# Output kept by tokens, decays as sums of logarithms, and elementwise work moved to GpSimd in an attention and Mamba kernel

## The chip, the cores and the metric

One core of one Trainium2 chip runs the kernel. The metric is the device time in microseconds (us) of one execution. The engines are named here TensorE (PE, with its weight loads PEld), VectorE (DVE), ScalarE (ACT), GpSimd (POOL) and SyncE (SP, which issues the transfers).

## The reference

The input `x` is (4, 128, 32, 32) in float32: four batches of 128 channels by 1024 tokens. Two blocks follow one another.

```
# block 1: attention
h = group_norm(x, 8 groups)                  # per batch
q, k, v = h @ qkv_w.T + qkv_b                # 1024 tokens x 128
x = x + softmax(q k^T / sqrt(128)) v @ proj_w.T + proj_b
# block 2: Mamba-2 with squeeze-and-excitation
u = layer_norm(x over channels)
z, xBC, dt = u @ in_w.T                      # 128, 128+64+64, 4
xs, B, C = silu(causal_conv4(xBC));  dt = softplus(dt + dt_bias)
state = state * exp(dt*A) + dt * xs * B;  y = state . C + Dp * xs   # 4 heads of 32
y = y * silu(z);  y = y * rsqrt(mean(y*y) + eps) * rms_w
out = y @ out_w.T
att = sigmoid(relu(mean_tokens(out) @ se1.T + b1) @ se2.T + b2)
result = x + out * att
```

## The kernel before

Everything stays on chip between the input and the output. A batch's 1024 tokens are worked in two halves of 512 (index `n`, 0 or 1), each of four tiles of 128 tokens. In a step's name the digits are the half, the tile or the sub-step, the letter is the batch (a to d), and `@k` the matmul bank that it fills. One list, `ORDER`, written out in the source, names every step once. Each engine walks the whole list and issues the steps that are its own; semaphores (`wait`) carry the data dependences. So the list sets each engine's queue, and an engine serves its queue strictly in order.

**Attention.** `h` (normalized input), `h_hi` and `h_lo` (a split into two reduced-precision parts) and `q_hi`, `q_lo` feed three-product matmuls: `Q`, and `S` (scores, 128 x 512). `max`, `exp`, `T` (transpose), `pT` (copy), `PV` (product with the values), `inv` and `res` (division and addition to the residual, which lies by tokens in `res`) follow. `xob` adds the projection's bias to `res` beforehand. `h_lo` and `xob` run on VectorE.

**Mamba.** `stats`, `ln_ve`, `ln_pow`, `u_tok`, `UT` and `u` make the normalized tokens; `InX`, `InBC`, `InZ` and `Dt` project them; `conv_x` and `conv_bc` are four taps each; `sp0` to `sp17` are the softplus in nine small VectorE steps per half, the last of which gives `la`, the logarithm of the decay. The decay of one step is `dA = exp(la)`. It is split into two parts and put into rows (`dA_rows`), transposed (`DAT`), masked by head (`dA_T`), spread by `L` over a bank, and `l`, a scan on VectorE, multiplies it up. `Dec` computes the sums of `la` up to each token with 16 products of 32 columns, and `decay` takes their exponential. `G`, `m`, `U`, `st`, `stc`, `Yo`, `Y` are the chunked state recurrence; `y` adds its parts; `g` applies the gate.

**End of a batch.** `sq`, `Ss`, `ms`, `y_pow` give `y_rstd`, one number a token. The output is by channels, so that number has to become a row: `y_rows` (two VectorE steps), `YrT` (transpose), `y_T` (copy), `YrB` (four products), `y_b` (copy). `Out` is one 128 x 512 product; `o` multiplies it by `y_b` and sums it over the tokens. `SeA`, `hdn`, `SeB`, `tha`, `att` are the excitation. `XR` transposes the residual back to channels and `fin` adds it, into `y`, from where SyncE stores 256 KB a half. The next batch's `y` waits for that store:

```
elif kind == "y":
    wait(dve, yo_dx_ready, b, n + 1)
    wait(dve, out_sent[n], b - 1, 16)
```

GpSimd has `ln_pow`, `gate`, `xend`, `dx`, `yo_dx`, `g` and `y_pow`. The order staggers the batches: while batch b is in its Mamba part, the attention of batch b+1 runs; after the last attention, only Mamba is left. At the start the statistics of batches 1 to 3 (`gn_stats1`) stand in VectorE's queue between `h_lo1a` and `q_lo0a`, and `winC` is made (`win_mm`) before `Q0a`.

## Time and profile before

| | |
|---|---|
| median of 3 runs | 328.7 us (328.65 to 328.84) |
| the profiled execution's own time | 328.64 us |
| its span, first to last instruction | 326.9 us |
| mean granted TensorE clock | 0.974 |
| busy: PE, DVE, ACT, POOL | 284.5, 261.0, 187.3, 81.9 us |
| instructions | 6452 |

Busy time is the union of an engine's instructions. Matmuls are pipelined, and a record also covers its latency, so TensorE's busy time is more than its throughput needs; how far apart equal products start in a dense stretch is the better price. A float32 product appears as two records, a transpose or a reduced-precision product as one.

### The profile page before, as it was taken

The page shows a single profiled execution, that of the slowest core. Times are in us where ns is not written, and L with a number is a line of the kernel's source. Part 1 is how long each engine was busy: PE and PEld are TensorE (multiplying, and loading weights), DVE is VectorE, ACT ScalarE, POOL GpSimd, SP SyncE. Part 2 cuts the span into 40 slices and gives each one's busy share as a digit, 9 for nine tenths or more (in the row PEclk, how much of TensorE's full clock was granted, in tenths as well). Part 3 has the DMA queues.
Part 4 walks back from the last instruction along what each step waited for, and adds up shares of the span by engine and source line. Part 5 has one row for each costly group of instructions (what it writes and reads, how often), then busy time and mean ns, then how long its engine had stood idle before and what let it go on. Part 6 is the DMA issues. An engine that isn't in the chain of part 4 may idle for free.

```text
span 326.9 us, 6452 instructions
## 1 busy us (share of the span) xinstructions
PE 284.5 (87%) x2206; PEld 232.1 (71%) x2206; DVE 261.0 (80%) x586; ACT 187.3 (57%) x347; POOL 81.9 (25%) x99
## 2 busy tenths in 40 slices
PE   0598999999999999899999999999999988756663
PEld 0477897897879778676787877887987765445542
DVE  4674475997798978969989998988999988996523
ACT  1324577978786855666587656566574835641011
POOL 6000100001011025541502522162023176107340
PEclk9999999999999999999999999999999999996777
DMA  7900000000000000000000000000000010000101
GB/s 216 369 6 1 2 0 3 0 2 0 2 1 3 0 2 2 0 3 1 2 1 9 25 34 1 2 0 3 3 0 2 2 64 1 3 0 2 64 0 66
DMA packets 3791, 7.34 MB, mean 22 GB/s; under 512 B 656, under 2 KB 1584, under 8 KB 3760
## 3 DMA queue, kind: packets, MB, share of 16 engines
q1 hardware_dynamic: 3216, 6.72, 5.7%
q8 instruction: 19, 0.31, 0.4%
q10 hardware_dynamic: 544, 0.21, 0.2%
q14 instruction: 12, 0.10, 0.1%
HBM read 4.83 MB, written 2.10 MB: 21 GB/s over the span
## 4 chain that ended last, share of the span: by engine, by line
PE 57%; DVE 26%; issue 7%; ACT 4%; POOL 2%; DMA 2%; DVEq 1%; ACTq 0%; POOLq 0%
PE mamba L947 20%; PE attn_out L947 12%; PE scores L947 12%; PE turn L1015 6%; DVE L L872 4%; DVE pre L822 3%; DVE neg_max L784 3%; PE turn L947 2%; DMA out<-y 2%; DVE gn_raw L707 1%; PE mamba L1073 1%; DVE scanned L892 1%; DVE L L884 1%; DVE y L936 1%; DVE y L907 1%
## 5 line engine op out<-in xcount | busy, mean ns | idle before, releaser
L947 PE MATMUL attn_out<-values,pT 128*128 128x129 f32 x512 | 66.8, 276 | 0.3 <-DVE res L793 0.2
L947 PEld LDWEIGHTS attn_out<-values,pT 128*128 128x128 f32 x512 | 62.9, 191 | 4.2 <-issue 2.8
L533 ACT ACTIVATE probs<-scores,neg_max 128x512 f32<-128x512 f32 x64 | 42.8, 684 | 25.8 <-DVE neg_max L784 20.4
L784 DVE TENSOR_REDUCE neg_max<-scores 128x1 f32<-128x1024 f32 x32 | 39.0, 1218 | 15.5 <-PE scores L947 15.1
L539 ACT ACTIVATE pT<-turn 128x512 f32<-128x512 f32 x64 | 37.4, 594 | 14.4 <-PE turn L1015 8.9
L872 DVE TENSOR_TENSOR_SCAN L<-mamba,ident 128x512 f32<-128x512 f32 x32 | 38.2, 1212 | 2.3 <-PE mamba L947 2.1
L1015 PE MATMUL turn<-ident,probs 128*128 128x128 f32 x256 | 37.8, 273 | 0.0
L822 DVE SCALAR_TENSOR_TENSOR pre<-raw,vec,pre 128x512 f32<-128x512 f32 x48 | 37.5, 789 | 0.2
L947 PE MATMUL scores<-h_hi,q_hi 128*128 128x512 f32 x64 | 31.4, 491 | 3.4 <-ACT probs L533 2.5
L1015 PEld LDWEIGHTS turn<-ident,probs 128*128 128x128 f32 x256 | 30.2, 141 | 5.8 <-issue 3.3
L445 POOL TENSOR_TENSOR ln_rstd<-ln_var,neg_half 128x4 f32<-128x4 f32 x8 | 8.5, 1066 | 81.1 <-DVE ln_var L804 81.1
L463 POOL TENSOR_TENSOR xend<-xdt,to_end 128x512 f32<-128x512 f32 x8 | 9.8, 1228 | 74.3 <-DVE xdt L865 39.0
L947 PE MATMUL scores<-h_hi,q_lo 128*128 128x512 f32 x64 | 25.8, 404 | 0.0
L947 PE MATMUL mamba<-u,winC 128*128 128x512 f32 x48 | 24.9, 604 | 0.9 <-DVE L L872 0.4
L947 PE MATMUL scores<-h_lo,q_hi 128*128 128x512 f32 x64 | 25.6, 400 | 0.0
L884 DVE TENSOR_TENSOR L<-L,mamba 128x512 f32<-128x512 f32 x32 | 21.3, 678 | 1.0 <-PE mamba L947 1.0
L456 POOL TENSOR_TENSOR gate<-gate,zv 128x512 f32<-128x512 f32 x16 | 20.5, 1286 | 3.6 <-ACT gate L584 3.4
L947 PEld LDWEIGHTS scores<-h_hi,q_hi 128*128 128x128 f32 x64 | 12.3, 192 | 11.1 <-issue 7.6
L947 PE MATMUL mamba<-dA_head,pick_chunk 128*128 128x512 f32 x32 | 14.3, 468 | 2.4 <-ACT BT L616 0.6
L623 ACT ACTIVATE stateT<-scanned 128x512 f32<-128x512 f32 x8 | 9.2, 1145 | 12.1 <-DVE scanned L892 12.1
L484 POOL TENSOR_TENSOR xs<-y,gate 128x512 f32<-128x512 f32 x8 | 11.0, 1380 | 13.8 <-DVE y L907 13.8
L947 PEld LDWEIGHTS scores<-h_hi,q_lo 128*128 128x128 f32 x64 | 12.3, 192 | 2.9
(189 smaller groups left out, 572.1 us busy)
## 6 DMA issues: line engine op xcount, KB each, us to landing
res<-in_x_tok SPq DMA_DIRECT2D x4, 512.0 KB, 8.1
out<-y SPq DMA_DIRECT2D x8, 256.0 KB, 2.0
x_all<-in_x SPq DMA_DIRECT2D x3, 512.0 KB, 8.0
x_all<-in_x SPq DMA_DIRECT2D x2, 256.0 KB, 3.2
winT<-in_in_wT SPq DMA_DIRECT2D x1, 194.0 KB, 6.4
wqkv<-in_qkv_w ACTq DMA_DIRECT2D x1, 192.0 KB, 3.6
wpT<-in_proj_wT SPq DMA_DIRECT2D x1, 64.0 KB, 3.6
ob_row<-in_proj_b SPq DMA_DIRECT2D x1, 64.0 KB, 5.5
```

The source lines that it names most:

```text
L456: pool.tensor_tensor(gate[:, half], gate[:, half], zv[:, half], ALU.add if part else ALU.mult).then_inc(gate_ready.sem, 1)
L463: pool.tensor_tensor(xend[:, rows, :], xdt[:, rows, :], to_end[:, rows].unsqueeze(2).broadcast_to([P, R, HEADDIM]), ALU.mult).then_inc(xen ...
L484: pool.tensor_tensor(y2[:, half], y[:, half], gate[:, half], ALU.mult).then_inc(y2_ready.sem, 1)
L533: act.activation(probs[:, i % 2, half_of(h)], scores[:, half_of(h)], ACT.Exp, bias=neg_max[:, i:i + 1]).then_inc(exp_done.sem, 1)
L539: act.activation(pT[:, i % 2, QUAD * h:QUAD * (h + 1), :], bank[:, :].rearrange("p (a b) -> p a b", a=QUAD), ACT.Copy).then_inc(pT_ready.s ...
L623: act.activation(stateT[:, n, :, :], scanned[:, n, :, :].rearrange("s e c -> s c e"), ACT.Copy).then_inc(stc_ready.sem, 1)
L784: V.tensor_reduce(neg_max[:, n:n + 1], scores[:, :], AX.X, ALU.max, negate=True).then_inc(max_ready.sem, 1)
L822: V.scalar_tensor_tensor(pre[:, k, half_of(n)], raw[:, k, n * HALF + j:(n + 1) * HALF + j], vec[:, at + j:at + j + 1], pre[:, k, half_of(n ...
L872: V.tensor_tensor_scan(L[:, HEADS * n:HEADS * (n + 1), :].rearrange("p a b -> p (a b)"), bank[:, :], ident4[:, :, :].rearrange("p a b -> p ...
L884: V.tensor_tensor(M[:, HEADS * n:HEADS * (n + 1), :], L[:, HEADS * n:HEADS * (n + 1), :], bank[:, tile(c)].unsqueeze(1).broadcast_to([P, H ...
L947: return T.matmul(o, w, v, start=start, stop=stop)
L1015: last = T.transpose(bank[:, tile(c)], probs[:, i % 2, tile(QUAD * h + c)], ident[:, :])
```

## The change

The output by tokens. `Out` becomes four products that put tokens on the partitions, so `y_rstd` is one number a partition: `o` is four scaled copies on ScalarE. `y_rows`, `YrT`, `y_T`, `YrB`, `y_b`, `XR` and `att` go. The mean over tokens is now `os` (GpSimd adds pairs of tiles), `Pl` (two products with ones) and `pl` (a copy). `SeB` gives the excitation broadcast over the partitions, with its bias as a 33rd row; `gated` (VectorE) multiplies, into the spent `x_all`; `fin` adds it to `res`, on GpSimd for batches 0 to 2 and on VectorE for the last; the store goes from `res`, 256 KB a half with 2 KB pieces a partition as before, and the host puts the result back by channels.

The decays. `Cum` computes the sums of `la` for the 16 columns with one product, `dec` takes the exponential on ScalarE, and it travels in `dA_rows` beside `dA`, through `DAT` and `dA_T`; `Dec` is then one product 512 wide with `head_sel`, and `decay` is a copy. `cd` reads its sums from `Cum`'s bank.

VectorE's work on GpSimd: `xob` and `h_lo` for batches 1 to 3.

The head: `gn_bs1` to `gn_bs3` are the statistics in three pieces; `win_mm` comes after `S1a`; `kq_mm` after `gn_mm20`; the whole order is a new one. A kind `warm`, products on idle TensorE, is defined, but the order does not contain it.

```
 ORDER = """
+gn_stats0 gn_mm10 vp_mm gn_dev0 gn_mm20 kq_mm gn_ve0 vp_ev gn_pow0 gn_aff0 win_s h_hi0a xob0a h0a h_hi1a h_lo0a h1a
+kq_ev Q0a h_lo1a V0a@0 q_hi0a gn_bs3 Q1a q_lo0a q_hi1a gn_bs1 S0a v0a V1a@1 q_lo1a v1a gn_bs2 S1a win_mm max0a
+gn_stats1 exp0a gn_mm11 exp1a S2a T0a@1 S3a pT0a T1a@1 max1a PV0a pT1a gn_dev1 PV1a exp2a exp3a T2a@1 alog S4a win_ev
...
+max6c L0b@2 PV5c stats0c exp12c Yo1a@0 inv2c l0b exp13c S14c yo1a S15c h_hi0d res2c yo_dx1a L1b@2 pT9c max7c Y1a@1
+h_hi1d h_lo0d L2b@0 th_bc1b PV6c exp14c silu1b PV7c pT10c y1a l1b th_x1b InZ1b@1 g1a stats1c L3b@2 xs0b h_lo1d zv1b
+Q0d stats2c zt1b inv3c T11c@1 res3c gate0b l2b Cum1b@1 exp15c PV8c dec1b q_hi0d dA_rows1b Q1d stats3c pT11c l3b PV9c
...
+yo_dx0d U1d@1 m4d dx1d st1d fin0c m5d stc1d Y0d@1 m6d Yo1d@2 y0d m7d g0d yo1d Y1d@2 yo_dx1d sq0d Out0d@1 y1d Ss0d@2
+g1d ms0d y_pow0d sq1d Ss1d@0 o0d ms1d Out1d@0 y_pow1d os0d o1d Pl0d@2 pl0d os1d fin1c Pl1d@0 pl1d SeA0d@1 hdn0d
+SeB0d@0 tha0d gated0d gated1d fin0d fin1d
@@ setup on VectorE
+            rows = ident[:, 0:4 * R].rearrange("r (s k c h) -> r k s c h", s=2, k=2, c=QUAD)
+            for k in range(2):
+                V.tensor_reduce(row_head[:, k, :], rows[:, k].rearrange("r s c h -> r h s c"), AX.XY, ALU.add)
+                last = V.tensor_reduce(row_chunk[:, k, :], rows[:, k].rearrange("r s c h -> r c s h"), AX.XY, ALU.add)
+            V.tensor_copy(head_sel[:, :, :], row_head[:, 1, :].unsqueeze(2).broadcast_to([P, HEADS, HEADDIM]))
+            step_done(V.tensor_tensor(head_mask[:, :, 1:P], row_head[:, 0, :].unsqueeze(2).broadcast_to([P, HEADS, P - 1]),
+                                      row_chunk[:, 1, :].unsqueeze(2).broadcast_to([P, HEADS, P - 1]), ALU.add))
@@ GpSimd
+                elif kind == "xob" and b > 0:
+                    pool.tensor_tensor(res[:, b, four, :], res[:, b, four, :],
+                                       ob_row[:, :].unsqueeze(1).broadcast_to([P, QUAD, P]), ALU.add
+                elif kind == "h_lo" and b > 0:
+                    pool.tensor_tensor(h_lo[:, half], h32[:, half], h_hi[:, half].bitcast(F32), ALU.subtract
+                elif kind == "os":
+                    pool.tensor_tensor(o_sum[:, n, :, :], o_tok[:, QUAD * n:QUAD * n + 2, :],
+                                       o_tok[:, QUAD * n + 2:QUAD * (n + 1), :], ALU.add)
+                elif kind == "fin" and b < BATCH - 1:
+                    pool.tensor_tensor(res[:, b, four, :], res[:, b, four, :], gated(b, n), ALU.add
@@ ScalarE
-                    act.activation(decay_in[:, half], bank[:, :], ACT.Exp, scale=1.0 / A_SCALE
+                    act.activation(decay_in[:, half], bank[:, :], ACT.Copy)
+                elif kind == "dec":
+                    act.activation(dA[:, n, R:2 * R], bank[:, 0:R], ACT.Exp, scale=1.0 / A_SCALE)
-                elif kind == "y_b":
+                elif kind == "o":
+                    for c in range(QUAD):
+                        last = act.activation(o_tok[:, i, :], bank[:, tile(c)], ACT.Copy, scale=y_rstd[:, i:i + 1])
@@ VectorE
                 elif kind == "y":
-                    wait(dve, out_sent[n], b - 1, 16)
+                    wait(dve, gated_ready, b - 1, n + 1)
+                    wait(dve, o_sum_ready, b - 1, n + 1)
+                elif kind == "gated":
+                    V.scalar_tensor_tensor(gated(b, n), th_att[:, :].unsqueeze(1).broadcast_to([P, QUAD, P]), 1.0,
+                                           o_tok[:, QUAD * n:QUAD * (n + 1), :], ALU.add, ALU.mult)
@@ TensorE
-                        for h in range(HEADS):
-                            last = mm(bank[h * HEADDIM:(h + 1) * HEADDIM, tile(c)],
-                                      la[:, n, r:r + 1].broadcast_to([P, HEADDIM]), upto[:, :])
+                elif kind == "Cum":
+                    mm(bank[:, 0:R], upto[:, :], la[:, n, :])
+                    mm(bank[:, R:2 * R], ones[:, :], la[:, n, :]).then_inc(done, 1)
+                elif kind == "Dec":
+                    mm(bank[:, :], head_sel[:, :, :].rearrange("r h d -> r (h d)"),
+                       dA_head[:, n, :, :].rearrange("r h i -> r (h i)")).then_inc(done, 1)
-                    mm(bank[:, :], woutT[:, :], y2[:, half]).then_inc(done, 1)
+                    for c in range(QUAD):
+                        last = mm(bank[:, tile(c)], y2[:, tile(QUAD * n + c)], woutT[:, :])
+                elif kind == "Pl":
+                    mm(bank[:, 0:1], o_sum[:, n, 0, :], ones[:, 0:1], True, False)
+                    mm(bank[:, 0:1], o_sum[:, n, 1, :], ones[:, 0:1], False, True).then_inc(done, 1)
-                elif kind == "XR":
```

## Rows read from the trace of the kernel before

**Rows 1.** The page: busy time of each engine, share and instructions.

```profile
PE 284.5 (87%) x2206; PEld 232.1 (71%) x2206; DVE 261.0 (80%) x586; ACT 187.3 (57%) x347; POOL 81.9 (25%) x99
```

**Rows 2.** Busy time by stretch: window, length, each engine's busy us, clock, DMA share, GB/s.

```profile
27.80:72.00 44.20, 42.56 (x312) 36.74 (x313) 30.59 (x81) 31.83 (x58) 1.87 (x2) 1.00 0.00 1
72.00:115.80 43.80, 43.10 (x286) 35.96 (x285) 36.99 (x78) 33.77 (x64) 3.57 (x3) 1.00 0.01 1
115.80:187.70 71.90, 67.56 (x602) 55.53 (x601) 64.03 (x132) 47.81 (x88) 26.67 (x24) 1.00 0.02 5
187.70:262.00 74.30, 72.26 (x608) 60.78 (x608) 68.35 (x159) 47.06 (x90) 19.37 (x18) 1.00 0.02 5
262.00:290.00 28.00, 22.41 (x202) 14.77 (x200) 25.07 (x58) 14.96 (x30) 12.40 (x10) 1.00 0.06 20
290.00:327.00 37.00, 21.28 (x154) 15.96 (x154) 18.90 (x37) 5.42 (x10) 12.00 (x12) 0.77 0.08 29
```

**Rows 3.** The chain that ended last, in the head: start, us, what.

```profile
17.18 3.58 DVE gn_raw L707 x6
21.78 1.50 PE scores L947 x3
...
24.92 1.63 PE scores L947 x3
...
28.67 0.94 PE scores L947 x3
```

**Rows 4.** The same chain in dense stretches, for the spacing of products.

```profile
123.22 0.87 PE turn L1015 x8
...
154.75 0.70 PE scores L947 x3
155.45 0.86 PE mamba L947 x2
...
158.41 1.08 PE mamba L947 x32
```

**Rows 5.** Groups of VectorE instructions: busy us, mean ns; idle before, releaser.

```profile
L936 DVE SCALAR_TENSOR_TENSOR y<-y,att,mamba 128x512 f32<-128x512 f32 x8 | 5.9, 743 | 0.4 <-PE mamba L1156 0.3
L776 DVE TENSOR_TENSOR h_lo<-h,h_hi 128x512 fp32r<-128x512 f32 x8 | 5.5, 686 | 1.4 <-ACT h L510 1.2 <-ACT h_hi L516 0.2
L926 DVE CUSTOM_DVE_ANT_0 y<-mamba,th 128x512 f32<-128x512 f32 x8 | 5.5, 682 | 1.2 <-PE mamba L947 1.0 <-ACT th L631 0.2
L921 DVE CAST y_T<-mamba 128x128 fp32r<-128x128 f32 x8 | 2.3, 285 | 4.5 <-PE mamba L1131 4.5
L671 DVE CAST y_rows<-y_rstd 128x4 fp32r<-128x4 f32 x8 | 1.3, 158 | 0.1
```

**Rows 6.** Groups of ScalarE and GpSimd instructions, the same columns.

```profile
L456 POOL TENSOR_TENSOR gate<-gate,zv 128x512 f32<-128x512 f32 x16 | 20.5, 1286 | 3.6 <-ACT gate L584 3.4
L546 ACT ACTIVATE u_tok<-res,ln_rstd 128x128 f32<-128x128 f32 x32 | 10.2, 395 | 2.7 <-POOL ln_rstd L445 2.7
L631 ACT ACTIVATE th<-mamba 128x512 f32<-128x512 f32 x8 | 4.8, 596 | 9.3 <-PE mamba L947 9.3
```

**Rows 7.** Two lines of VectorE: duration ns min/median/max, first and last start.

```profile
L693 DVE SCALAR_TENSOR_TENSOR sp_log<-sp_sum,sp_s x8: 149/176/1061, 60.5 to 277.0; 128x16 f32<-128x16 f32 x8
L822 DVE SCALAR_TENSOR_TENSOR pre<-raw,vec,pre x48: 720/746/1598, 61.0 to 287.1; 128x512 f32<-128x512 f32 x48
```

**Rows 8.** The chain that ended last, from 262 us on.

```profile
262.31 2.01 DMA out<-y
...
301.24 0.65 PE mamba L1156 x4
...
308.14 2.04 DMA out<-y
...
310.27 0.70 DVE y L907
...
313.08 3.52 PE mamba L947 x10
```

More of the change, by code:

```diff
@@ L392, in _ @@
                 for n in range(2):
-                    wait(sp, fin_ready, b, n + 1)
-                    sp.dma_start(out_d[b][:, half_of(n)], fin[:, half_of(n)]).then_inc(out_sent[n].sem, 16)
+                    four = slice(QUAD * n, QUAD * (n + 1))
+                    if b == BATCH - 1:
+                        wait(sp, fin_last, 0, n + 1)
+                    else:
+                        wait(sp, fin_ready, b, n + 1)
+                    sp.dma_start(out[b][:, four, :], res[:, b, four, :]).then_inc(out_sent[n].sem, 16)
             for n in range(2):
@@ L831, in step @@
                     if k == SP_STEPS - 1:
-                        wait(dve, filled["Dec"], b - 1, n + 1)
-                        wait(dve, filled["DAT"], b - 1, n + 1)
+                        wait(dve, filled["Cum"], b - 1, n + 1)
+                        wait(dve, dA_ready, b - 1, n + 1)
                     softplus(b, n, k).then_inc(sp_step.sem, 1)
@@ L855, in step @@
                     wait(dve, filled["L"], b - 1, QUAD * (n + 1))
+                    wait(dve, filled["Dec"], b - 1, n + 1)
                     bank = take(dve, b, "DAT", n)
@@ L1127, in step @@
                     last.then_inc(done, 1)
-                elif kind == "YrT":
-                    wait(pe, y_rows_step, b, 2 * n + 2)
-                    bank, done = fill(pe, b, "YrT", n)
-                    T.transpose(bank[:, 0:P], y_rows[:, n, :], ident[:, :]).then_inc(done, 1)
-                elif kind == "YrB":
-                    wait(pe, y_T_ready, b, n + 1)
-                    bank, done = fill(pe, b, "YrB", n)
-                    for c in range(QUAD):
-                        last = mm(bank[:, tile(c)], pick_row[:, c:c + 1].broadcast_to([P, P]), y_T[:, n, :])
-                    last.then_inc(done, 1)
                 elif kind == "Out":
@@ L1150, in step @@
                     bank, done = fill(pe, b, "SeB", 0)
-                    mm(bank[:, 0:1], se2T[:, :], hdn[:, :]).then_inc(done, 1)
-                elif kind == "XR":
-                    wait(pe, res_ready, b, QUAD * (n + 1))
-                    bank, done = fill(pe, b, "XR", n)
-                    for c in range(QUAD):
-                        last = T.transpose(bank[:, tile(c)], res[:, b, QUAD * n + c, :], ident[:, :])
-                    last.then_inc(done, 1)
+                    mm(bank[:, 0:P], hdn[0:SE + 1, :].broadcast_to([SE + 1, P]), se2T[:, :]).then_inc(done, 1)
             for kind, n, b, _ in STEPS:
```

356 lines of the change are left out of this document (183 added, 173 removed).

## The prediction

> **What bounds the kernel now.** I read the page's busy line first, then the span cut at the five points where the order of the work changes, then the chain of waits, then single groups. TensorE and VectorE are both near full: 284.5 and 261.0 us of 326.9 us [rows 1]. Averages hide that they take turns. The cuts are the first `exp` of batches 0 to 3, the last `PV`, and the end of the dense part [rows 2]. Up to 115.8 us the matmul records cover 85.7 of 88.0 us while VectorE has 67.6: TensorE sets the pace. From 115.8 to 262 us the next batch's attention runs beside the Mamba part of the one before: VectorE 132.4 of 146.2 us, with a gap behind each of 291 instructions, and TensorE 139.8 us. Both bind there, and matmul records overlap, so VectorE is the tighter. From 262 to 290 us there is no attention left and VectorE alone is dense (25.1 of 28.0). In the last 37 us nothing is: a chain of dependent steps sets the end, at a mean granted clock of 0.77.
>
> The forecast is a sum against the profiled execution's own 328.64 us (its span of 326.9 plus 1.74 around it); the median of the runs, 328.7, is 0.06 above it, so the same sum serves.
>
> **Part 1, the head.** Today six normalization statistics of batches 1 to 3 stand on the chain for 3.58 us, between the first `Q` and `q_lo0a` [rows 3]. The change puts them in three pieces behind other work, and moves the four-way product for `winC` from ahead of `Q0a` to behind `S1a`. But TensorE is slow here: three score products take 1.50 us at 21.8 us and 0.94 us at 28.7 us [rows 3], so it is at the lower level of its two (1.2 against 2.4 GHz), although the granted-clock column still says 1.00. Freed of the statistics, the six groups Q, V, Q, S, V, S stand back to back for six times about 1.5 us = 9 us from about 16.8 us: about 25.8 us for the second half of the scores, against 26.55 us now. The setup on VectorE grows: four reduces for two, `head_sel` one more copy, the mask an addition instead of a copy, about +0.6 us, in front of everything. `winC` then fills the 2 us of maximum and exponential. I take -1 us, between +1 (setup costs more, `winC` delays `S2a`) and -3 (TensorE rises earlier because it has no hole, as at 28.7 us).
>
> **Part 2, TensorE.** Per half of a batch: `Dec` was 16 products on 32 columns of the array, 1.08 us [rows 4]; it becomes one product as wide as a scores product, of which three take 0.70 us [rows 4], so 0.23. `YrT` goes (0.11, as one of eight transposes in 0.87 [rows 4]), `YrB` goes and `XR` goes (four each, 0.44 each by the same spacing). Added: `Cum`'s product with `upto` (two short records, 0.2) and `Pl` (four records, 0.4). `Out` is two wide records, 0.86 [rows 4], and becomes eight narrow ones, 0.87 by the row of the transposes. Sum per half: -0.85 -0.11 -0.44 -0.44 +0.2 +0.4 = -1.2 us, eight times about -10 us.
>
> **Part 3, VectorE.** Per half: out go `o` (0.68), `fin` (0.74), `y_T` (0.29) and two `y_rows` (0.16 each) [rows 5]; in come `gated` (like `fin`, 0.74) and `pl` (0.16, like `y_rows`): -1.1 us. For batches 1 to 3 `h_lo` and `xob` go to GpSimd: twelve of 0.68 [rows 5] = -8.2 us. For the last batch `fin` stays as two additions (0.68 each), +1.4. In all about -16 us.
>
> **Part 4, the price on ScalarE and GpSimd.** On ScalarE `y_b` (0.60 [rows 6]) is replaced by `o` as four scaled copies, each like `u_tok`: 32 in 10.2 us, so four in 1.28 [rows 6]; with `dec` (0.2) about +0.9 us per half, +7 us on an engine with 187 of 327 us [rows 1]. Hidden by its own idle time, except at the end, where it is counted below. GpSimd gets 18 wide two-input operations (six `xob`, six `h_lo`, six `fin`) of 1.29 us as `gate` [rows 6], and eight `os` of half the width, between 0.65 and 1.29 us, I take 0.7: +29 us on 82. It does not fill it. But it collides. Steps of the softplus that take 0.18 us take 1.06 us now and then, and taps of the convolution go from 0.75 to 1.60 us [rows 7]; in the trace these are the ones issued while a GpSimd operation runs. Mean less median: 2.1 us over the 48 taps, 1.7 us over the 8 of the row shown, and four other softplus lines do the same (some 1.4 us each): 9.5 us lost against some 68 us of GpSimd work. In proportion, 29 us more cost 4 us; between 0 (the new ones meet operations that read the matmul buffers) and 8 (the taps alone are 36 us of VectorE's 261, all open to it).
>
> The Trainium skill, page SBUF — State Buffer, section Who interferes with whom, says that a VectorE instruction with two SBUF inputs and a GpSimd instruction that reads SBUF exclude each other for the whole instruction, whoever starts second waiting. The trace agrees with it: 1.06 us where 0.18 is usual [rows 7]. By that rule `h_lo`, `xob` and `fin` don't leave VectorE for nothing, and the sum would move towards its dearer end.
>
> **What this is worth from 28 to 262 us.** Up to 115.8 us the pace is TensorE's, which sheds there only 1.3 us (both `Dec` of batch 0, less their `Cum`); VectorE loses 7 us in that stretch (six `xob`, four `h_lo`), which can shorten TensorE's 2.3 us of idle time: -2. From 115.8 to 262 us TensorE sheds about 6 us (five halves at 1.2), and VectorE about 7 (five halves at 1.1, two `h_lo`): I take -6.5 for the pair. Collisions give back +3 of the 4. Together -5.5 us, between 0 and -11.
>
> The decays also get a longer path: `Cum`, then an exponential, then the rows, where the exponential of `la` went straight into the rows; `Dec` now stands behind `dA_T`. That is about 0.8 us of latency per half. It is covered while the engines are dense; uncovered it would cost 0.8 us for batch 3, which is inside the ranges.
>
> **Part 5, from 262 us.** Three times the chain runs through a store, the first at 262.3 us: `fin` writes where the next batch's `y` must go, and `y` waits for the transfer, 2.0 us [rows 8]. After the change the result lies in `res`, and `y` waits for `gated`, long done. At the last one, 308.1 to 310.2 us, VectorE has nothing else: 2.1 us [rows 8]. The first two are half filled with other work, and with 1.8 us less VectorE work in the stretch I take -2 for 262 to 290 us (0 to -4). Further, `XR0c` at 301.2 us (0.65 [rows 8]) and `fin0c` (0.74) stand on the chain before the last `Yo` products, for want of a bank: -1.2 of their 1.4.
>
> The last chain runs from `y1d`, done at 311.0 us [rows 8], to the end. Out of it go the `y_rows` pair (0.32), `YrT` and `YrB` with their latency (0.9), `y_T` (0.29), `y_b` (0.60) and `o` (0.68): 2.8 us. Into it come `o` on ScalarE (1.3), `os` (0.7), `Pl` and `pl` (0.6), and two passes more at the end, since `gated` and `fin` are two operations where one was (2 x 0.68): 4.0 us. The sums of squares and `Out`, 3.52 us at the half level of the clock [rows 8], need `Out` no longer ahead of the rest of the chain, and are 0.9 us for eight records at the full level: -1 to -2.6, I take -2. Together -0.8, with one semaphore step fewer -1, between -3 and +1. Sum after 290 us: -2.1 -1.2 -1 = -4.3 us, between -8 and -1.
>
> **Sum:** -1 -5.5 -2 -4.3 = -12.8 us, 328.6 - 12.8 = **315.8 us**.
>
> **Rivals.** (A) *The forecast*, 310.5 to 320 us. (B) *GpSimd gives the middle back.* The gain from 28 to 262 us is eaten by collisions and by `h_lo` at 1.29 in place of 0.68 us; only the ends stay: -7.3 us, 321.3 us. For it: [rows 7], and both engines bound there. Against: GpSimd idle two thirds of the time. (C) *Everything pays.* The middle yields TensorE's whole saving and more, -10, the head -3, the rest -7: 308.6 us. For it: VectorE is the tighter engine in the middle, and it loses the most. Against: the price of the collisions. (D) *Slower: GpSimd's queue becomes the path.* It is served in order; `h_lo1d` stands behind `g1a`, which waits for `y1a`, and `Q1d` with every score of batch 3 waits for `h_lo1d`; likewise for batches 1 and 2. If each of the three starts is held by over 4.3 us, the 12.8 us are gone and the kernel is slower; at 6 us each it takes 334 us. For it: the order ties two batches on one queue, and GpSimd's mean operation there is long, 1.29 us [rows 6]. Against: the scores are doubly fed, TensorE has other work there. (E) *The clock.* With 10 us less work for TensorE the half level, which now shows as a mean of 0.77 over the last 37 us [rows 2], spreads: doubling some 4 us of products costs as much again, 319.8 us; it lies within A's edge. (F) *Nothing*: gains and prices cancel within 0.2%.
>
> **How the numbers follow.** A with E 0.50, B 0.20, C 0.18, D 0.08, F 0.04. The time is A's. The range 307 to 323 us holds A, most of B (its own spread is 319.5 to 326) and the nearer two thirds of C, about 0.8. A measurement of this kernel can tell about 0.2% from no change: faster 0.88, same 0.04, slower 0.08.
>
> **What would show it.** Right: no wait of `y` for a store; statistics off the chain before the first `q_lo`; one record per `Dec`; VectorE's busy time near 248 us, GpSimd's near 111, ScalarE's near 194, TensorE's records down by over 10; `exp` of batch 3 near 180 us and the last `PV` near 255. Wrong: softplus steps of 1 us by the dozen, with VectorE's busy time hardly down (B); ScalarE or TensorE waiting for `h_lo` on GpSimd for several us (D); the last `PV` still at 262 us; a last stretch at 0.5 of the clock. The weakest step is the middle: what two full engines yield when each loses a few per cent depends on the order, which sums don't show.

## The result, and the profile after

The kernel after takes 316.75 us (median of four, 314.55 to 318.24), the one before 328.77 us beside it (328.65 to 329.86): ratio 0.9622, 95% interval 0.9554 to 0.9689, so 12 us faster. The profiled execution took 314.55 us with a span of 312.8 us; it is the fastest of the four. A second measurement of the same kernel, made as a control beside the first experiments, gave 316.63 us and a ratio of 0.9625 [0.9596, 0.9655]; its profiled span is 316.0 us. That two profiles of one kernel differ by 3.2 us is a finding of its own, below, and single spans have to be read with it in mind.

The page, busy time of each engine; it answers to [rows 1]:

```profile
PE 270.7 (87%) x1982; PEld 227.0 (73%) x1982; DVE 247.5 (79%) x541; ACT 193.5 (62%) x379; POOL 110.9 (35%) x125
```

VectorE, ScalarE and GpSimd are where they were forecast (248, 194, 111). What TensorE's records cover fell by 13.8 us. The span, cut at the same events as [rows 2] (first `exp` of batches 0 to 3, start of the last `PV`, then 279 us); columns as there:

```profile
24.14:64.70 40.56, 39.69 (x269) 34.27 (x269) 22.47 (x63) 27.89 (x50) 8.17 (x7) 1.00 0.01 1
64.70:109.98 45.28, 43.63 (x291) 36.70 (x291) 38.01 (x83) 36.18 (x71) 9.38 (x9) 1.00 0.00 1
109.98:168.51 58.53, 55.86 (x421) 46.50 (x420) 51.34 (x111) 41.62 (x80) 18.77 (x17) 1.00 0.01 2
168.51:250.86 82.35, 78.79 (x615) 67.48 (x615) 74.19 (x159) 54.78 (x116) 33.09 (x31) 1.00 0.02 8
250.86:279.00 28.14, 21.48 (x175) 16.16 (x174) 25.43 (x54) 17.61 (x36) 16.26 (x14) 0.93 0.05 20
279.00:312.80 33.80, 20.74 (x171) 16.56 (x169) 19.98 (x30) 8.54 (x19) 19.36 (x18) 0.80 0.08 32
```

The new order moves work between the stages: batch 3 starts its scores 58.5 us after batch 2 instead of 72, and the last attention takes 82 us instead of 73 or so. Single stages can't be compared, so the sum is made over four pieces. In the profile of before, the first `exp` starts at 27.84 us, the last `PV` at 261.18 and the last `y` at 310.27 [rows 8]. Here all four lengths are from the profiled executions:

| piece | before | after | control | change (control) | forecast |
|---|---|---|---|---|---|
| start to the first `exp` | 27.84 | 24.14 | 24.84 | -3.7 (-3.0) | -1 |
| first `exp` to the last `PV` | 233.34 | 226.72 | 226.67 | -6.6 (-6.7) | -5.5 |
| last `PV` to the last `y` | 49.09 | 46.55 | 48.70 | -2.5 (-0.4) | -5.3 |
| last `y` to the end | 16.63 | 15.39 | 15.79 | -1.2 (-0.8) | -1 |

The middle piece is the same in both profiles to 0.05 us. The head and the tail are not. That holds for the kernel before too: a profile of it with the store's wait removed, which changes nothing in the head, has its first `exp` at 26.25 us instead of 27.84. Against that one the head gained 2.1 us (control 1.4), not 3.7.

The middle, from the first `exp` to the last `PV`, first of the kernel before, then of the kernel after:

```profile
27.84:261.18 233.34, 224.66 (x1795) 188.19 (x1795) 199.10 (x444) 159.87 (x297) 51.49 (x47) 1.00 0.01 4
```

```profile
24.14:250.86 226.72, 217.97 (x1592) 184.96 (x1592) 186.01 (x414) 160.47 (x314) 69.41 (x63) 1.00 0.01 4
```

TensorE's cover fell by 6.7 us and the stretch by 6.6: its idle time was 8.7 us and is 8.8. VectorE shed 13.1 us, twice as much, and its idle time rose from 34.2 to 40.7 us. The reader should see here which of two "full" engines was the bound: the one whose saving shows in the length.

The chain of waits in the head; [rows 3] stood here:

```profile
16.33 1.65 PE scores L998 x3
...
19.55 0.72 PE scores L998 x3
...
21.77 1.19 DVE gn_raw L769 x2
22.96 1.16 DVE neg_max L841
```

The six statistics are not gone from the chain (two stand on it for 1.19 us) but the 3.58 us became 1.19. What was not foreseen is the second row: three score products take 0.72 us at 19.6 us, the full level of the clock, where the kernel before still took 1.50 at 21.8 us.

The end of the chain, which answers to [rows 8]:

```profile
294.04 0.70 DVE y L968
...
294.87 1.11 POOL xs L509
...
296.10 1.29 POOL th L505
...
297.41 0.70 DVE y L968
```

No transfer stands in it any more. But in the place of the 2.04 us of the store stand `g0d` (line 509) and `yo_dx1d` (line 505), one behind the other in GpSimd's queue, and the last `y` waits for the second. From one `y` to the other it was 3.50 us and is 3.37.

GpSimd's new groups, in the columns of [rows 5], and the product that `Dec` has become:

```profile
L464 POOL TENSOR_TENSOR h_lo<-h,h_hi 128x512 fp32r<-128x512 f32 x6 | 8.1, 1356 | 8.4 <-ACT h_hi L554 8.4
...
L998 PE MATMUL mamba<-dA_head,head_sel 128*128 128x512 f32 x8 | 4.1, 514 | 0.0
```

And three lines of VectorE on which the collisions with GpSimd show, in the columns of [rows 7]; the first and the last are the lines that stood there:

```profile
L745 DVE SCALAR_TENSOR_TENSOR sp_log<-sp_sum,sp_s x8: 157/177/568, 62.6 to 267.5; 128x16 f32<-128x16 f32 x8
L735 DVE TENSOR_TENSOR sp_s<-sp_s,dte x8: 150/172/1308, 60.7 to 265.4; 128x16 f32<-128x16 f32 x8
L881 DVE SCALAR_TENSOR_TENSOR pre<-raw,vec,pre x48: 723/742/1095, 64.6 to 279.8; 128x512 f32<-128x512 f32 x48
```

The medians are unchanged. The long ones sit on other lines than before: `sp_log` now reaches 0.57 us where it reached 1.06, the taps 1.10 where they reached 1.60, while a step `sp_s` (line 735), at most 0.51 us before, reaches 1.31.

### The profile page after: what moved, and what is told of

Same layout as the page of the kernel before. It is cut to its first block, busy times and chain, and to the rows that moved or that the text cites. A ratio compares the mean times of both kernels' runs of the same rounds, so it can differ in the third digit from the quotient of the medians.

```text
span 312.8 us, 6092 instructions
## 1 busy us (share of the span) xinstructions
PE 270.7 (87%) x1982; PEld 227.0 (73%) x1982; DVE 247.5 (79%) x541; ACT 193.5 (62%) x379; POOL 110.9 (35%) x125
## 4 chain that ended last, share of the span: by engine, by line
PE 48%; DVE 25%; issue 13%; POOL 7%; ACT 6%; DVEq 1%; POOLq 0%; ACTq 0%
PE mamba L998 14%; PE scores L998 12%; PE attn_out L998 11%; PE turn L1070 6%; DVE L L932 4%; DVE neg_max L841 3%; DVE pre L881 2%; PE turn L998 1%; ACT probs L571 1%; PE mamba L1088 1%; DVE y L968 1%; PE mamba L1135 1%; DVE scanned L952 1%; DVE res L852 1%; POOL y_rstd L514 1%
## 5 line engine op out<-in xcount | busy, mean ns | idle before, releaser
L841 DVE TENSOR_REDUCE neg_max<-scores 128x1 f32<-128x1024 f32 x32 | 39.0, 1219 | 14.2 <-PE scores L998 13.8
L881 DVE SCALAR_TENSOR_TENSOR pre<-raw,vec,pre 128x512 f32<-128x512 f32 x48 | 36.0, 756 | 1.0 <-ACT pre L604 0.8
L998 PE MATMUL scores<-h_hi,q_hi 128*128 128x512 f32 x64 | 29.6, 463 | 1.6 <-ACT probs L571 0.9
L505 POOL TENSOR_TENSOR th<-th,sq 128x384 f32<-128x384 f32 (+1 forms) x8 | 9.9, 1234 | 33.3 <-DVE th L961 33.2
L509 POOL TENSOR_TENSOR xs<-y,gate 128x512 f32<-128x512 f32 x8 | 10.2, 1279 | 17.1 <-DVE y L968 17.1
L998 PE MATMUL mamba<-dA_head,pick_chunk 128*128 128x512 f32 x32 | 15.7, 504 | 0.4 <-DVE scanned L952 0.2
L514 POOL TENSOR_TENSOR y_rstd<-ms,neg_half 128x4 f32<-128x4 f32 x8 | 9.0, 1124 | 16.1 <-DVE ms L971 15.9
```

Of the source, the lines that this page charges most:

```text
L505: pool.tensor_tensor(yo[:, part], yo[:, part], dx[:, part], ALU.add).then_inc(yo_dx_ready.sem, 1)
L509: pool.tensor_tensor(y2[:, half], y[:, half], gate[:, half], ALU.mult).then_inc(y2_ready.sem, 1)
L514: pool.tensor_tensor(y_rstd[:, four], ms[:, four], neg_half[:, four], ALU.pow).then_inc(y_rstd_ready.sem, 1)
L841: V.tensor_reduce(neg_max[:, n:n + 1], scores[:, :], AX.X, ALU.max, negate=True).then_inc(max_ready.sem, 1)
L881: V.scalar_tensor_tensor(pre[:, k, half_of(n)], raw[:, k, n * HALF + j:(n + 1) * HALF + j], vec[:, at + j:at + j + 1], pre[:, k, half_of(n ...
L998: return T.matmul(o, w, v, start=start, stop=stop)
```

## The experiments

The kernels were measured in three groups, each on one chip and with its own runs of the kernel before (medians 329.36, 330.21 and 330.25 us), so across groups the ratio to the kernel before is compared; 0.001 is 0.33 us. The control is the kernel after at 0.9625. A difference of two ratios is uncertain by 1.3 to 1.7 us, and each profile is one execution.

| kernel | us | ratio, 95% interval | first `exp` | first `exp` to last `PV` |
|---|---|---|---|---|
| before + no wait for the store | 325.83 | 0.9896 [0.9865, 0.9927] | 26.25 | 233.30 |
| before + head reordered | 328.51 | 0.9959 [0.993, 0.9987] | 24.60 | 235.14 |
| before + `h_lo`, `xob` on GpSimd | 330.76 | 1.0049 [1.0019, 1.008] | 28.91 | 233.61 |
| control (after) | 316.63 | 0.9625 [0.9596, 0.9655] | 24.84 | 226.67 |
| after, `h_lo`, `xob` on VectorE | 318.14 | 0.965 [0.9613, 0.9688] | 24.89 | 228.10 |
| the same, and `fin` on VectorE | 318.05 | 0.9632 [0.9596, 0.9668] | 25.22 | 228.71 |
| after, `Dec` in 16 products | 319.63 | 0.9695 [0.9655, 0.9734] | 24.16 | 229.54 |
| after + idle-time products, head | 315.24 | 0.9556 [0.9518, 0.9595] | 23.89 | 226.85 |
| after, head in the old order | 319.80 | 0.9677 [0.9649, 0.9705] | 25.61 | 228.02 |
| after, last `y` freed | 315.98 | 0.9586 [0.9546, 0.9626] | 24.84 | 226.77 |
| both of these aids | 313.93 | 0.9523 [0.9481, 0.9566] | 22.77 | 226.85 |
| and idle-time products, tail | 313.74 | 0.9511 [0.948, 0.9543] | 23.53 | 226.89 |

### One part alone, on the kernel before

**The wait for the store.** `fin` writes into the spent slot of `x_all` and the store goes from there; all else is as before.

```
-                    sp.dma_start(out_d[b][:, half_of(n)], fin[:, half_of(n)]).then_inc(out_sent[n].sem, 16)
+                    sp.dma_start(out_d[b][:, half_of(n)], fin_of(b, n)).then_inc(out_sent[n].sem, 16)
 elif kind == "y":
-                    wait(dve, out_sent[n], b - 1, 16)
+                    wait(dve, fin_ready, b - 1, n + 1)
```

> The kernel before, with one thing changed: fin writes its result into the batch's own spent slot of x_all and the store leaves from there, so y of the next batch no longer waits for a transfer. By the prediction's terms: the three stores leave the chain, 2.1 us at 308 us and up to 2 us between 262 and 290 us, so 324.6 to 326.7 us. Rival: the wait only uncovers the bank or the product behind it, under 1 us, 328 us.

-3.4 us (2.4 to 4.4), as expected. The last `y` now starts 0.1 us after its product; the chain of this kernel near it:

```profile
307.32 1.05 PE mamba L950 x32
308.50 0.70 DVE y L910
...
311.32 2.02 PE mamba L950 x10
```

From `y0d` to `y1d` it is 1.86 us where it was 3.50, 1.6 us less. The two earlier stores gave 0.3 us: a tap of the convolution behind them starts 16.4 us after the last `PV` instead of 16.7. The last row is the same ten products that took 3.52 us in [rows 8]: this execution had the full level of the clock there, and its last chain takes 15.00 us against 16.63. In the three profiles that keep the wait (before and the two runs below) that chain takes 16.6 to 16.9 us and its sums of squares are at the half level. One profile can't show that the wait is the reason, but all six runs without it have a mean clock of 0.964 to 0.980, and 15 of the 18 runs of before have 0.954 to 0.960. Against this, the same profile is at the half level for longer between 282 and 300 us, so that the piece from the last `PV` to the last `y` is hardly shorter (48.95 us, 49.09 before). The span of this profile is 3.4 us shorter as well, but 1.6 of that is its earlier first `exp`, which the change doesn't touch.

**The head.** The statistics in three pieces and `win_mm` behind `S1a`, in the old order otherwise.

```
-h_lo0a xob0a h_lo1a gn_stats1 Q0a V0a@1 q_hi0a q_lo0a gn_mm11 v0a ...
+h_lo0a xob0a h_lo1a Q0a V0a@1 q_hi0a gn_bs3 q_lo0a v0a gn_bs1 Q1a S0a q_hi1a alog q_lo1a gn_bs2 S1a V1a@1 win_mm
+max0a gn_stats1 exp0a gn_mm11 ... pT0a S3a T1a@1 max1a gn_dev1 gn_mm21 PV0a
```

> The kernel before, with the head alone reordered: the statistics of batches 1 to 3 in three pieces behind q_hi0a, q_lo0a and q_lo1a, and the product for winC behind V1a. After the full change the first exp came 3.7 us earlier. Theory: most of it is this reordering, because TensorE has no hole and reaches its full clock earlier; the first exp comes 3 to 4 us earlier, and as TensorE sets the pace up to 116 us, nearly all of that arrives at the end: 325 to 326 us. Rival: the head's gain is absorbed by the dense middle, where VectorE is the bound and has the same work to do: 327.5 to 328.7 us.

-1.3 us (0.4 to 2.3), the rival's side, although the first `exp` came 3.2 us before that of the profile of before (1.7 us before that of the kernel without the wait). The loss stands in one place, which the chain of this kernel shows:

```profile
27.84 1.23 DVE neg_max L791
...
29.56 0.17 DVE gn_dev L725
...
29.78 0.39 PE mamba L954 x2
30.16 1.89 PE attn_out L954 x16
```

`gn_mm21` waits on TensorE for VectorE's statistics, and this kernel put it in front of `PV0a`, which starts 5.6 us after the first `exp` instead of 3.6: the piece from the first `exp` to the last `PV` is 1.8 us longer than before. That was a fault of my order, not a limit of the middle. In the change `gn_mm21` comes later, and the run with the old head, below, is the better test.

**The split on GpSimd.** Twelve operations leave VectorE and nothing else changes.

```
-                    V.tensor_tensor(h_lo[:, half], h32[:, half], h_hi[:, half].bitcast(F32), ALU.subtract
+                    pool.tensor_tensor(h_lo[:, half], h32[:, half], h_hi[:, half].bitcast(F32), ALU.subtract
```

> The kernel before, same order, with h_lo and xob of batches 1 to 3 on GpSimd instead of VectorE: 8.2 us less on VectorE, 15 us more on GpSimd. Theory: xob and two batches' h_lo lie where TensorE sets the pace and yield little, and the last h_lo pair yields 1.4 us: 326 to 328 us. Rival 1: VectorE binds everywhere and all 8 us arrive, 321 us. Rival 2: GpSimd's queue holds the scores of the next batch, slower than 329 us.

Slower by 1.6 us (0.6 to 2.6), outside the expectation. Its page:

```profile
PE 285.7 (87%) x2206; PEld 233.8 (71%) x2206; DVE 256.2 (78%) x574; ACT 187.5 (57%) x347; POOL 96.9 (29%) x111
```

VectorE is down by 4.8 us where twelve operations of 0.68 us would be 8.2, and the middle piece is 233.61 us against 233.34: nothing of it was gained. In this profile 1.1 us of the loss is the later first `exp` (28.91 instead of 27.84). It isn't the clock: the spacing of the products is that of before, at the half level up to the first `exp`. It is a collision in the head, where `xob` of batch 1 starts on GpSimd just before VectorE's own of batch 0:

```profile
15.80 1.30 POOL L451 TENSOR_TENSOR res<-res,ob_row 128x512 f32<-128x512 f32 x1 [3.49 <-DMA res<-in_x_tok]
15.89 1.75 DVE L789 TENSOR_TENSOR res<-res,ob_row 128x512 f32<-128x512 f32 x1
```

The same VectorE addition took 0.69 us before. The 1.06 us more pass through the statistics and `q_lo0a` to the second `Q` (22.71 us instead of 21.64) and to the first `exp`. In the old kernel, then, this swap buys nothing: 5 us less on VectorE, 15 us more on GpSimd, and `h_lo` at 1.3 instead of 0.68 us. It doesn't test less work on VectorE by itself. The second rival had the sign, but its mechanism, scores held by GpSimd's queue, doesn't show in the lengths: the middle is 0.3 us longer.

### One part undone, on the kernel after

**The same work back on VectorE**, first `h_lo` and `xob` of batches 1 to 3, then also the six `fin`:

```
-                    pool.tensor_tensor(h_lo[:, half], ...
+                    V.tensor_tensor(h_lo[:, half], ...
...
-                    pool.tensor_tensor(res[:, b, four, :], res[:, b, four, :], gated(b, n), ALU.add
+                    V.tensor_tensor(res[:, b, four, :], res[:, b, four, :], gated(b, n), ALU.add
```

> The changed kernel with h_lo and xob of batches 1 to 3 back on VectorE, the order unchanged: VectorE +8.2 us less what it no longer loses to collisions (3.4 us in the reverse experiment), GpSimd -15.7 us. Theory after that experiment, which moved them the other way in the old order and won nothing: within 1.5 us of the changed kernel, 315 to 318 us. Rival, by the prediction's sum: the middle is bound by VectorE and the 5 us net arrive, 320 to 322 us.

> As e1, and the six fin of batches 0 to 2 on VectorE too (4 us there, 7.6 us off GpSimd). Theory: VectorE's queue is in order and the batch 1 and 2 fin lie in its densest stretch, so about +2 us over e1: 317 to 320 us. Rival: GpSimd's queue was what held yo_dx and xs (g) near the end, and taking fin out of it makes the end earlier: at or below e1.

By the ratio the first costs 0.8 us, inside the intervals; the middle piece says it more sharply, since it repeats to 0.2 us in six profiles with the same middle: 228.10 against 226.7, +1.4 us. The middle of the first, and its `h_lo`:

```profile
24.89:252.99 228.10, 217.86 (x1593) 185.03 (x1593) 193.45 (x426) 160.51 (x314) 54.66 (x51) 1.00 0.01 4
```

```profile
L833 DVE TENSOR_TENSOR h_lo<-h,h_hi 128x512 fp32r<-128x512 f32 x6 | 5.2, 860 | 1.1 <-ACT h_hi L542 1.1
```

VectorE has 7.4 us more there, TensorE the same cover; a fifth of VectorE's extra time reaches the length. The run also takes 15 us off GpSimd, and `h_lo` takes 0.86 us there instead of 1.36, which may hide a part of VectorE's price; no run separates them. With `fin` as well the middle is 228.71 and the time is no longer (0.9632), the rival's side: `fin` on GpSimd is worth about half a microsecond in the middle, and nothing that the time shows.

**`Dec` in 16 products again**, with the exponential in `decay` (the last softplus step also waits for `Dec` again, which reads `la`):

```
-                    mm(bank[:, :], head_sel[:, :, :].rearrange("r h d -> r (h d)"),
-                       dA_head[:, n, :, :].rearrange("r h i -> r (h i)")).then_inc(done, 1)
+                    for c in range(QUAD):
+                        for h in range(HEADS):
+                            last = mm(bank[h * HEADDIM:(h + 1) * HEADDIM, tile(c)],
+                                      la[:, n, r:r + 1].broadcast_to([P, HEADDIM]), upto[:, :])
```

> The changed kernel with the 16 products of 32 columns back in Dec (and the exponential in decay), everything else and the order unchanged: TensorE +0.85 us eight times, 6.8 us. Theory: TensorE binds in part of the middle and on the last stretch only lightly, so about half arrives, +2 to +4 us: 319 to 321 us. Rival 1: all of it arrives, 323 to 324 us. Rival 2: TensorE has slack everywhere in the new order, under 1 us, 316 to 317.5 us.

+2.3 us by the ratio (0.7 to 3.9), within the theory. The middle piece and the group that came back:

```profile
24.16:253.70 229.54, 222.24 (x1779) 188.65 (x1778) 186.36 (x414) 160.57 (x314) 69.35 (x63) 1.00 0.01 4
```

```profile
L999 PE MATMUL mamba<-upto,la 128*32 128x128 f32 x256 | 9.2, 288 | 0.0
```

TensorE's cover rises by 4.3 us in the middle and its length by 2.8: two thirds of what TensorE is given is paid, against a fifth of what VectorE is given. This is the nearest to a direct comparison of the two engines.

**The head in the old order**, in the kernel after:

```
-kq_ev Q0a h_lo1a V0a@0 q_hi0a gn_bs3 Q1a q_lo0a q_hi1a gn_bs1 S0a v0a V1a@1 q_lo1a v1a gn_bs2 S1a win_mm max0a
-gn_stats1 exp0a
+kq_ev win_mm Q0a h_lo1a V0a@0 q_hi0a gn_bs3 gn_bs1 gn_bs2 gn_stats1 Q1a q_lo0a q_hi1a S0a v0a V1a@1 q_lo1a v1a S1a max0a
+exp0a
```

> The kernel after with the head in the old order: all statistics of batches 1 to 3 in front of q_lo0a, winC's products ahead of Q0a. Nothing else is changed. Theory (the head's order is worth at the end what it is worth at the first exp, 3.2 to 3.7 us, now that the middle is bound by TensorE): 2.5 to 3.7 us slower than the kernel after. Rival (as with the head alone in the kernel before, the middle takes most of it back): 0.5 to 1.5 us slower.

Slower by 1.7 us by the ratio (0.4 to 3.1) and by 3.2 us by the medians, between the two expectations; the last `PV` starts at 253.63 us, 2.1 us after the control's and 2.8 after the profile of after. I take 2 to 3 us for the head. Of this 1.3 us isn't in the head itself but between the first `exp` and the first `PV` (4.9 us instead of 3.6): `win_mm` keeps TensorE busy from 13.9 us and it reaches the full level early, but then it stands idle for 2.0 us before `S2a`, waiting for `exp0a`, and the clock falls again. Windows of 2 us of this kernel (the clock is the third number from the end):

```profile
26.00:28.00 2.00, 1.55 (x5) 1.19 (x6) 0.00 (x0) 0.88 (x2) 0.00 (x0) 0.66 0.00 0
28.00:30.00 2.00, 2.00 (x8) 1.56 (x7) 0.00 (x0) 0.60 (x1) 0.00 (x0) 0.50 0.00 0
```

### The clock and the last `y`

**Products without use in the head**, ten before `gn_mm10` and eight after `kq_mm`, of `ident` with itself:

```
-gn_stats0 gn_mm10 vp_mm gn_dev0 gn_mm20 kq_mm gn_ve0
+gn_stats0 warm10 gn_mm10 vp_mm gn_dev0 gn_mm20 kq_mm warm8 gn_ve0
```

> The changed kernel with products on idle TensorE in the head: ten 128 x 128 products ahead of gn_mm10 and eight behind kq_mm. Two profiles of one and the same kernel differ by 0.7 us at the first exp and keep that difference to the last PV; runs with the same head differ by up to 2.7 us there, so the moment at which TensorE reaches its full clock is worth that much. Theory: with these products it is at the full level when Q0a starts, the first exp comes at about 22.5 to 23.5 us instead of 24.1 to 24.8, and the end 1 to 2 us earlier with less spread: 314.5 to 315.5 us. Rival: the products delay gn_mm10 or the chain behind it, no gain, 316 to 318 us.

-2.3 us by the ratio (0.7 to 3.9), -1.4 by the medians, the expected sign. TensorE's timeline in this kernel:

```profile
11.62 2.03 PE L998 MATMUL scores<-ident 128*128 128x128 f32 x16
15.85 0.55 PE L998 MATMUL scores<-h_hi,key_query_hi 128*128 128x512 f32 x1 [2.20 <-DVE col L793]
...
18.62 0.77 PE L998 MATMUL scores<-h_hi,key_query_hi 128*128 128x512 f32 x1
...
19.60 0.40 PE L998 MATMUL scores<-h_hi,key_query_lo 128*128 128x512 f32 x1
```

The products lift the clock but can't hold it: `Q0a` begins fast, the rest of it is slow again after 2.2 us of idling, and full level returns at 19.6 us. The first `exp` is 0.3 to 1.0 us earlier than in the two profiles of after. So not all of the 2.3 us are accounted for by the trace. The expectation took 2.7 us between runs with one head for the clock's doing; 1.1 us of them were the collision above, and 1.6 are left.

**The last `y` freed.** `Y1d` goes to another bank than `Yo1d`, and the last `yo_dx` runs on VectorE:

```
-... Yo1d@2 y0d m7d g0d yo1d Y1d@2 yo_dx1d ...
+... Yo1d@2 y0d m7d g0d yo1d Y1d@0 yo_dx1d ...
+                elif kind == "yo_dx" and (n, b) == (1, BATCH - 1):
+                    V.tensor_tensor(yo[:, half], yo[:, half], dx[:, half], ALU.add).then_inc(yo_dx_ready.sem, 1)
```

> The kernel after, with two edits for the last half of the last batch alone: the product Y1d goes to another bank than Yo1d, and the sum yo + dx runs on VectorE instead of GpSimd. Theory (the last y of the kernel is held by GpSimd's sum, which ends at 297.38 us, 0.03 us before y starts, and by the shared bank): on VectorE the sum takes 0.68 us where GpSimd takes 1.28, and it can start as soon as yo is written, so y starts 0.6 to 1.2 us earlier and the kernel is 0.6 to 1.2 us faster than the one after (about 315.5 to 316 us against 316.6). Rival (VectorE's own queue holds it just as long): within 0.3 us of the kernel after.

-1.3 us by the ratio, uncertain by 1.6 and so not resolved by the times, -0.65 by the medians. The timeline:

```profile
297.67 0.69 DVE L966 TENSOR_TENSOR th<-th,sq 128x512 f32<-128x512 f32 x1
...
298.40 0.69 DVE L972 TENSOR_TENSOR y<-mamba,th 128x512 f32<-128x512 f32 x1
```

`y` now follows its sum directly. From `y0d` to `y1d` it is 2.72 us, against 3.37 in the profile of after and 4.02 in the control, whose last `Y` products ran at the half level of the clock. So at the full level the two edits gain 0.65 us, the lower edge of what was expected. The piece from the last `PV` to the last `y`, 46.79 us, is no shorter than in the profile of after (46.55), because the clock before it was lower (a mean of 0.85 against 0.89).

**Both together**, and then with 56 products more in the tail, ahead of eleven that wait there (`warm8 Cum1d`, `warm6 Out1c`, `warm8 Pl0c`, `warm4 G1d`, `warm8 Y0d`, `warm6 Y1d`, `warm4 Ss1d`, `warm2 Out1d`, `warm3 Pl0d`, `warm5 Pl1d`, `warm2 SeA0d`):

> The two edits of the tail together with the 18 idle-time products in the head. Theory (the two act at different ends of the kernel and add up): 2.5 to 3.5 us faster than the kernel after, 313 to 314 us. Rival (what is won in the head comes back as an earlier fall of the clock in the tail): no more than 1.5 us faster than the kernel after.

> As the run before, with 56 more products without use, put into TensorE's queue ahead of eleven products of the last 45 us that wait for other engines (2 to 8 each, filling about as much as the idle time seen there). Theory (the half level of the clock in the last stretch costs time on the path: the sums of squares of the last half take 1.16 us for eight there and 0.6 at the full level, the last Y, Out and Pl likewise): the granted clock stays at the full level after 270 us, and the time falls by 1 to 3 us against the run before. Rival (these products are too short beside the vector operations between them, and the useless ones delay them): within 0.5 us, or slower.

The first is 3.4 us faster than the control by the ratio (1.7 to 5.1), within what was expected if the two aids add up. The second is at 0.9511 against 0.9523, the rival's side. The last 63 us of it, cut at the last `y`:

```profile
250.42:298.51 48.09, 43.04 (x380) 35.24 (x379) 42.19 (x77) 22.34 (x44) 27.98 (x25) 0.93 0.05 18
298.51:313.80 15.29, 9.33 (x78) 8.59 (x77) 3.83 (x9) 3.44 (x11) 5.92 (x6) 0.91 0.13 52
```

The clock is up (0.93 and 0.91), though not all the way: it was at the half level from 284 to 290 us. And the last chain takes 15.29 us, against 15.39 at a mean of 0.78 in the profile of after. The traces show why it had so little to win. In the profile of after TensorE is at the full level in that chain up to about 306 us; the half level behind that covers one short group of products (`SeB`, 0.79 us against 0.49 here) and then time in which TensorE has no work. The sums of squares of the last half, first in the profile of before, then of after:

```profile
313.08 1.81 PE L947 MATMUL mamba<-ones,sq 128*128 128x128 f32 x8 [0.85 <-ACT sq L627]
...
300.23 1.16 PE L998 MATMUL mamba<-ones,sq 128*128 128x128 f32 x8 [0.85 <-ACT sq L669]
```

The expectation had 1.16 us for the half level and 0.6 for the full one; but 1.16 is the full level, and it is 1.16 in this run too. On the other side the products without use stand on the path themselves, here in the chain of this kernel (`scores` is where they write):

```profile
295.99 1.34 PE scores L1002 x12
297.33 1.05 PE mamba L1002 x32
298.51 0.70 DVE y L972
```

From `y0d` to `y1d` it is 3.44 us where it was 2.72, and from the last `PV` to the last `y` 48.09 where the run before has 45.90 in its profile. By the times the two kernels are level, and both beat the kernel before and the one after.

## Why the prediction was right, and where it was not

**The forecast.** 315.8 us against a median of 316.75, faster as said. Its sum, -12.8, meets the profiled -14.1 and the measured -12.0. By pieces it was less good: the head and the middle were too small and the tail up to the last `y` too large (-5.3 against -2.5, in the control -0.4), and they cancelled. That the sum comes so near the time is in part luck.

**Part 1, the head: too small.** -1 was forecast; -3.7 and -3.0 are in the profiles (-2.1 and -1.4 against the other execution of the old head), and 2 to 3 us came back when the head was put in the old order. The sum had six groups at about 1.5 us each, that is, all at the lower level. `Q0a` was (1.65 us for three), but the next `Q` was not (0.72); in the control it still was (1.29), and the full level came with `S0a`. The bound of -3 named this reason, a TensorE without a hole rising earlier; the value taken left it out.

**Part 2, TensorE: right.** It was to shed 1.3 us up to batch 2 and some 6 us to the last `PV`, 7.3 in all; its cover fell by 6.7. The first two stages together went from 88.0 us to 85.8, near the forecast -2, though the new order moves work across their end. `Dec` alone is 2.8 us of the middle's length, where its six halves there at 0.85 us are 5.1: its cover shows 4.3 of them, the length 2.8.

**Part 3, VectorE: the step that failed.** "Both bind there, and matmul records overlap, so VectorE is the tighter." The runs show the opposite. Middle length follows TensorE's cover to 0.1 us in the change; +4.3 us for TensorE costs 2.8, +7.4 us for VectorE costs 1.4, and -5 us for VectorE in the old kernel, traded for 15 us on GpSimd, gave nothing. Gaps behind 291 VectorE instructions [rows 2] were its slack, not its latency. The forecast of the middle was still close because the term for "the pair" was sized by TensorE's 6 us, and because the +3 for collisions, which didn't come, made up for gains of -8.5 that were 1.9 too large.

**Part 4, the collisions: too large.** +3 us were charged. Over ten short lines (the nine of the softplus and `to_end`) VectorE spent 24.7 us before and 24.1 after, and on the taps 37.5 and 36.0 us, with 29 us more on GpSimd. Over all of VectorE's groups of four and more, the time above each group's median is 13.4 us before and 13.2 after, and every one of the 18 and 22 instructions that lie over 0.1 us above it overlaps one of GpSimd. The long steps moved to other lines, and what they cost didn't grow. Proportion to GpSimd's busy time was the wrong rule: what counts is which instruction of the list meets which. The split measured alone shows a price on VectorE itself (4.8 of 8.2 us saved; 2.0 of the missing 3.4 are one addition of 1.75 us, shown above, and a longer step of `dA_rows`); undone in the kernel after, `h_lo` takes 0.86 us on VectorE instead of 0.69, so the collision is then met from the other side. The Trainium skill, page SBUF — State Buffer, section Who interferes with whom, has VectorE's second port pair shared with GpSimd as an exclusive lock; both of these are what it would lead one to expect.

**Part 5, from 262 us: the last store right, the rest not.** Removing the wait alone gives 3.4 us by the times. Its profile has 1.6 us of it at the last store, where 2.1 were charged, 0.3 at the two earlier ones, which with 1.8 us less VectorE work were to give -2, and 1.6 in the last chain, by the level of the clock. The -1.2 for `XR0c` and `fin0c` doesn't show: the kernel before with the wait removed needs 48.95 us from the last `PV` to the last `y`, the control 48.70, at the same mean clock (0.83 and 0.82). The windows of the one, then of the other:

```profile
259.55:308.50 48.95, 38.32 (x318) 27.99 (x316) 40.16 (x80) 18.00 (x34) 20.76 (x19) 0.83 0.05 17
```

```profile
251.51:300.21 48.70, 39.05 (x300) 30.20 (x299) 41.68 (x76) 22.64 (x44) 29.71 (x26) 0.82 0.05 17
```

So up to the last `y` the rest of the change brings about nothing. One reason is shown: the stall of the last `y` was filled by GpSimd's `yo_dx1d`, behind `g0d` in the same queue; freeing it gives 0.65 us. The prediction had GpSimd's mean of 1.29 us and its order at hand and did not ask what is late next there. The last chain measures -1.2 and -0.8 where -1 was forecast, but not by a shorter form. With its products at the full level of the clock the old form takes 15.00 us (without the store's wait) and the new one 15.29 to 15.39; the old one took 16.63 in the profile of before because its sums of squares and its first `Out` met the half level. The prediction had both sides of this, +1.2 of steps and -2 from the level; measured are +0.3 to +0.4 and -1.6. No run separates the new form's parts.

**The rivals.** B (the middle gives nothing) fell with the middle's -6.6. C (everything pays) was near in the head and wrong in the tail. D (GpSimd's queue) did not come at the starts of the batches: VectorE and TensorE have no wait for `h_lo` there. It came, small, at the last `y`. E (the clock) named the right object; in the head the change has no more time at the half level than before. In the tail, before and after have the same mean clock within 0.01 up to the last `y` in the profiled executions (0.90 and 0.89), but the control has 0.82.

**What is left.** By the ratios: the store 3.4, the head 2 to 3 with `Dec` 2.3, the split about 0.8, `fin` nothing: some 9 us of 12. Each of these is uncertain by 1 us or more, so the remaining 3 us are not sharply known. The middle piece says it better: of its 6.6 us, `Dec` is 2.8, the split 1.4 and `fin` 0.6, and 1.8 us stay open between the transposes and products of `XR`, `YrT` and `YrB` that went, the VectorE work that went with them, and the new order of the middle; no run took them apart.

## What to carry to other kernels

Where two engines are both over 85% busy, cut out the stretch between two fixed events and compare its length with each engine's cover in a version that sheds work on one of them: the bound is the engine whose saving shows, and work taken off the other is worth a fraction of it. When a wait on a path goes, list what else the waiting instruction needs and when each of these is ready: here the wait was worth 1.6 us between the last two `y`, and GpSimd's queue took all but 0.1 of it. Before explaining a mean clock, look where in the stretch it is low, since the half level costs nothing while TensorE has no work. In a head where TensorE starts at the half level, close its holes before shortening anything else: it pays twice, once as idle time and once as the clock.

## What the runs showed of the hardware

**The moment at which the clock rises differs between executions of the same head.** `Q0a` starts within 0.01 us in the two profiles of after (16.33 and 16.32), but the second `Q` is at the full level in one and at the half level in the other. Timeline of TensorE, first after, then the control:

```profile
19.30 0.48 PE L998 MATMUL scores<-h_hi,key_query_hi 128*128 128x512 f32 x1
19.62 0.39 PE L998 MATMUL scores<-h_lo,key_query_hi 128*128 128x512 f32 x1
```

```profile
19.33 0.77 PE L998 MATMUL scores<-h_hi,key_query_hi 128*128 128x512 f32 x1
19.90 0.63 PE L998 MATMUL scores<-h_lo,key_query_hi 128*128 128x512 f32 x1
```

The difference of 0.70 us at the first `exp` is still 0.65 at the last `PV`. In two profiles with the head of before, the first `exp` is at 26.25 and 27.84 us, again with the first `Q` within 0.01 us; 1.6 us, and the middle behind it differs by only 0.04. (The 28.91 us of the split alone is the collision above.) The Trainium skill, page TensorE: Matmul & The Clock Gate, Part 1, says that one kernel shows different numbers of slow products at its start from run to run; the trace agrees: the second `Q`'s products start 0.32 and 0.24 us apart in one execution, 0.57 and 0.43 in the other.

**The same happens in the tail.** From the last `PV` to the last `y` the mean clock is 0.89 in the profile of after and 0.82 in the control, and the stretch takes 46.55 and 48.70 us. In windows of 1 us, after is at the half level from 275 to 282 and from 285 to 289 us, the control from 277 to 290 and from 294 to 297. Here the row of after:

```profile
250.86:297.41 46.55, 35.64 (x300) 27.39 (x299) 41.58 (x75) 22.70 (x44) 29.69 (x26) 0.89 0.05 18
```

Head and tail together make the spread of about 1% that the times of this kernel show. It hides effects under 1 us from single spans; the lengths between fixed events in the dense middle repeat to 0.05 us in the two profiles of after and to 0.2 over six with the same middle, and resolved parts (the split, `fin`) that the times did not.

**An instruction of VectorE can wait out one of GpSimd.** The addition of 0.69 us that took 1.75 us ended 0.5 us after the GpSimd operation beside it (15.80 to 17.10 us, 15.89 to 17.64), and the long softplus steps all overlap a GpSimd instruction.
